# 66 columns of the edge sort on TensorE, attention head by head with its quotients on ScalarE

## What is computed

```
xn = layernorm(x)
# 1. graph part: edge softmax over each source, messages both ways
e     = exp(w - max(w, 0));  row_sum = segment_sum(e, src)
att   = e / (row_sum[src] + 1e-6)
M     = xn @ Wm + bm
out0  = segment_sum(att * M[dst], src);  out1 = segment_sum(att * M[src], dst)
g     = relu(relu(layernorm([out0 out1] @ W1 + b1)) @ W2 + b2), zero where row_sum == 0
# 2. linear attention, 8 heads of 64
q = softmax(xn Wq + bq), k = softmax(xn Wk + bk)  (over the 64 of a head), v = xn Wv + bv
context = k^T v (64 x 64 a head);  D_inv = 1 / (q . sum_t k)
mix = (q context * D_inv + q) @ Wp + bp
x = x + g + mix
# 3. experts: each row goes to one of 8 FFNs (512 -> 256 -> 512, gelu), times its router's probability
x = x + ffn(layernorm(x))
```

## Time and profile before

| | us |
|---|---|
| median of 3 runs (lowest, highest) | 497.45 (495.84, 501.89) |
| the profiled execution's own time | 500.75 |
| its span, first to last instruction | 498.7 |
| PE, PEld busy | 424.8, 347.8 |
| DVE, ACT, POOL busy | 380.7, 266.9, 208.9 |
| TensorE's mean granted clock | 0.955 of full speed |

### The profile page before, as it was taken

One profiled execution on the slowest core, in us unless ns is written; L12 is line 12 of the kernel. 1 busy time (PEld: TensorE's weight loads), 2 busy tenths in 40 slices (PEclk: granted clock), 3 DMA queues, 4 the chain that ended last, 5 costly groups with the idle time before them and its releaser, 6 DMA issues.

```text
span 498.7 us, 8596 instructions
## 1 busy us (share of the span) xinstructions
PE 424.8 (85%) x2637; PEld 347.8 (70%) x2637; DVE 380.7 (76%) x790; ACT 266.9 (54%) x739; POOL 208.9 (42%) x157
## 2 busy tenths in 40 slices
PE   4189999999998999975777777899898857999992
PEld 1167888888877887964555555799876745788881
DVE  6979979999978886963999999478379973455652
ACT  0686667776662222740667777654335661566550
POOL 0588888688886888992000000000000007255322
PEclk9699999999999999995999999999999857999998
DMA  7980000000000000005000000000006964233210
GB/s 196 312 289 3 1 3 3 3 3 2 3 2 3 1 3 2 2 2 185 3 1 2 2 2 1 2 0 1 1 0 258 411 214 126 74 114 111 69 63 17
DMA packets 15584, 31.06 MB, mean 62 GB/s; under 512 B 7494, under 2 KB 8125, under 8 KB 14517
## 3 DMA queue, kind: packets, MB, share of 16 engines
q1 hardware_dynamic: 9237, 23.21, 13.6%
q0 software_dynamic: 6304, 7.30, 7.3%
HBM read 24.90 MB, written 7.37 MB: 65 GB/s over the span
## 4 chain that ended last, share of the span: by engine, by line
PE 36%; POOL 35%; issue 11%; DVE 7%; ACT 5%; DMA 4%; SPq 1%; ACTq 0%; DVEq 0%; POOLq 0%
POOL slots L485 33%; PE banks L733 9%; PE banks L886 7%; PE banks L569 5%; PE banks L752 4%; ACT adj L1601 4%; PE banks L745 2%; DMA x_rows<-factors 2%; PE banks L877 2%; PE banks L702 1%; DVE stat L1337 1%; PE banks L818 1%; PE banks L725 1%; DMA rec<-x_rows,get_i 1%; DVE rec L1335 1%
## 5 line engine op out<-in xcount | busy, mean ns | idle before, releaser
L485 POOL DMA_INDIRECT slots<-record,row_i x112 | 167.3, 1494 | 38.5 <-issue 37.9
L496 POOL DMA_INDIRECT rec<-x_rows,get_i x17 | 18.6, 1092 | 188.8 <-DMA x_rows<-factors 183.9
L1601 ACT ACTIVATE adj<-banks x108 | 58.4, 589 | 39.5 <-PE banks L733 38.2
L569 PE MATMUL banks<-w_hi,xT_hi 128*125 128x512 f32 (+1 forms) x160 | 59.5, 372 | 0.7 <-DVE xT_lo L1088 0.6
L733 PE MATMUL banks<-d_hot,s_hot 128*128 128x251 f16 x432 | 59.9, 276 | 0.2
L569 PE MATMUL banks<-w_lo,xT_hi 128*125 128x512 f32 (+1 forms) x160 | 58.5, 366 | 0.0
L569 PE MATMUL banks<-w_hi,xT_lo 128*125 128x512 f32 (+1 forms) x160 | 58.5, 366 | 0.0
L1536 ACT ACTIVATE q_sb<-q_sb,hmax 125x64 f32<-125x64 f32 x80 | 26.7, 335 | 34.2 <-DVE hmax L1111 34.2
L733 PEld LDWEIGHTS banks<-d_hot,s_hot 128*128 128x128 f16 x432 | 33.4, 97 | 7.3 <-issue 0.3
L569 PEld LDWEIGHTS banks<-w_hi,xT_hi 128*125 128x125 f32 x160 | 29.7, 185 | 7.0 <-ACT xT_hi L1511 0.9
L505 POOL DMA_INDIRECT out<-o_sb,out_i x17 | 17.1, 1006 | 41.4 <-DVE o_sb L1441 41.4
(11 more groups left out here) (300 smaller groups left out, 1062.8 us busy)
## 6 DMA issues: line engine op xcount, KB each, us to landing
w_raw<-in_w2f SPq DMA_DIRECT2D x4, 1024.0 KB, 9.2
w_raw<-in_wqkv SPq DMA_DIRECT2D x3, 1024.0 KB, 17.5
rec<-in_x SPq DMA_DIRECT2D x2, 1120.0 KB
x_rows<-rec SPq DMA_DIRECT2D x10, 224.0 KB
w1a<-in_w1f SPq DMA_DIRECT2D x1, 2048.0 KB, 7.5
w1b<-in_w1f SPq DMA_DIRECT2D x1, 2048.0 KB, 16.5
b_sb<-in_b2f SPq DMA_DIRECT2D x1, 2048.0 KB, 22.2
slots<-record,row_i POOLq DMA_INDIRECT x112
```

Source lines behind the costliest of these rows:

```text
L485: pool.indirect_dma_start(slots, bass.IndirectOffsetOnAxis(ap=row_i[:, c:c + 1], axis=0), record[:, c, :], None).then_inc(slot_st, 16)
L569: mm = pe.matmul(dst, ab, cd, start=(i == 0), stop=(i == n - 1))
L1601: act.activation(adj[:, bass.ds(w, BW2)], flat_banks[0:TP, bass.ds(out_at, BW2)], ACT.Copy).then_inc(win_ok, 1)
```

## The change

- PCOLS goes from 58 to 66: POOL scatters 104 columns, PE sorts 33 pairs of columns instead of 29 (EARLY stays 6).
- k^T v goes head by head: eight matmuls of 64 stationary and 65 moving columns instead of four of 128 and 129. Even heads come out on PSUM partitions 0 to 63, odd ones on 64 to 127, all in bank 7. `ctxd` has 65 columns a head; its zeros go, and one copy on DVE and one on ACT bring it over instead of four each.
- The attention product goes head by head: eight matmuls with contraction 64 and 65 columns; even heads into one bank, odd ones into another.
- The quotients move from DVE to ACT: DVE takes the reciprocals of tile t+2 at the end of the loop of tile t (`attend`), ACT multiplies head by head (`divide`, eight activations of 125x64 out of PSUM a tile), and DVE adds q (`add_query`).
- The bias row and the router's column sums move behind the sort and RUN_UP, into banks 0 and 1, after PE has waited for `part_ok`; DVE takes them up behind its last batch. `wp_raw` therefore has to live longer, and `got`, `keys`, `parts` and `v_sb` get other places; the column of ones in `v_sb` is set once `w_lo` is made.

```diff
-PCOLS = 58
+PCOLS = 66
...
-        v_sb = place("v_sb", 26624, [TP, 2, KD, 129])
+        v_sb = place("v_sb", 5000, [TP, 2, H, DH + 1])
...
+        def ctx_at(h):
+            s = 64 * (h % 2)
+            return bank[7][s:s + 64, h // 2 * (DH + 1):(h // 2 + 1) * (DH + 1)]
+
+        def num_at(t, odd):
+            return bank[((3, 2), (4, 7))[t % 2][odd]][0:TP, 0:KD * (DH + 1)].rearrange("p (k n) -> p k n", k=KD)
...
@@ PE @@
-                for k in range(KD):
-                    kk = k_sb[:, r, k * 128:(k + 1) * 128]
-                    first, last = t == 0 and k == 0, t == NT - 1
-                    mm = pe.matmul(ctx_at(k), kk, v_sb[:, r, k, :], start=first or (t == 0 and k == 3), stop=last,
-                                   skip_group_check=True)
+                for h in range(H):
+                    mm = pe.matmul(ctx_at(h), k_sb[:, r, h * DH:(h + 1) * DH], v_sb[:, r, h, :],
+                                   start=(t == 0 and h < 2), stop=(t == NT - 1), skip_group_check=True)
...
-            bias_row(0)
-            bias_row(1)
             context(NT - 1)
...
             def attend(t):
                 if t >= 2:
                     pe.wait_ge(num_used, t - 1)
-                for k in range(KD):
-                    mm = pe.matmul(num_at(t, k // 2)[:, k % 2, :], qT[:, k, t * TP:(t + 1) * TP],
-                                   ctxd[:, k, :], start=True, stop=True)
+                for h in range(H):
+                    s = slice(64 * (h % 2), 64 * (h % 2) + 64)
+                    mm = pe.matmul(num_at(t, h % 2)[:, h // 2, :], qT[s, h // 2, t * TP:(t + 1) * TP], ctxd[s, h // 2, :],
+                                   start=True, stop=True)
                 mm.then_inc(num_ps, 1)
...
             attend(0)
             attend(1)
-            bias_row(2)
-            bias_row(3).then_inc(row_ps, 1)
             ao_turn(0)
...
             for _ in range(RUN_UP):
                 pe.matmul(bank[IDLE_IN][:, 0:WIN], ident, const("cols"), start=True, stop=True)
+            pe.wait_ge(part_ok, 2)
+            pe.wait_ge(ld_wp, 32)
+            for k in range(KD):
+                pe.matmul(bank[0][0:TP, :], bv_col[:, k:k + 1].to_broadcast([128, TP]), wp_raw[:, k, :], start=(k == 0),
+                          stop=(k == KD - 1))
+            pe.wait_ge(ld_small, 16)
+            for k in range(KD):
+                mm = pe.matmul(bank[1][0:TP, 0:E], ones[:, 0:TP], little("ws")[:, k * E:(k + 1) * E], start=(k == 0),
+                               stop=(k == KD - 1))
+            mm.then_inc(row_ps, 1)
...
@@ DVE @@
             def attend(t):
                 dve.wait_ge(num_ps, t + 1)
                 if t >= 2:
-                    dve.wait_ge(aoT_ps, t - 1)
...
+                    dve.wait_ge(num_used, t - 1)
+                for odd in range(2):
+                    last = dve.reciprocal(rden[:, t % 2, odd, :], num_at(t, odd)[:, :, DH])
+                last.then_inc(rden_ok, 1)
+
+            def add_query(t):
                 dve.wait_ge(num_used, t + 1)
                 dve.tensor_tensor(ao[:, t % 2, :], ao[:, t % 2, :], q_sb[:, t, :], ALU.add).then_inc(ao_ok, 1)
...
+            attend(0)
+            attend(1)
             for t in range(NT):
-                attend(t)
...
+                add_query(t)
                 if t >= 1:
                     aoT_split(t - 1)
...
                 if t >= 2:
                     mix_add(t - 2)
+                if t + 2 < NT:
+                    attend(t + 2)
...
@@ ACT @@
+            def divide(t):
+                act.wait_ge(rden_ok, t + 1)
+                if t >= 2:
+                    act.wait_ge(aoT_ps, t - 1)
+                for h in range(H):
+                    last = act.activation(ao[:, t % 2, h * DH:(h + 1) * DH], num_at(t, h % 2)[:, h // 2, 0:DH], ACT.Copy,
+                                          scale=rden[:, t % 2, h % 2, h // 2:h // 2 + 1])
+                last.then_inc(num_used, 1)
+
+            divide(0)
+            divide(1)
             for t in range(NT):
                 act.wait_ge(aoT_ps, t + 1)
...
+                if t + 2 < NT:
+                    divide(t + 2)
                 if t in SCALED:
                     act_parts(SCALED[t])
```

More of the change, by code:

```diff
@@ L257, in build @@
         hrec = sb("hrec", [TP, 2, H])
-        ctxd = sb("ctxd", [128, 4, 130])
-        rden = sb("rden", [TP, 2, 2, 2])
+        ctxd = sb("ctxd", [128, KD, DH + 1])
+        rden = sb("rden", [TP, 2, 2, KD])
         pr_i = sb("pr_i", [TP, 2, NB], I32)
@@ L290, in build @@
         flat_banks = banks[:, :, :].rearrange("p b n -> p (b n)")
-        def ctx_at(k):
-            return bank[7][:, k * 129:(k + 1) * 129] if k < 3 else bank[2][:, 0:129]
-        def num_at(t, half):
-            return bank[((3, 2), (4, 7))[t % 2][half]][0:TP, 0:260].rearrange("p (k n) -> p k n", k=2)
+        def ctx_at(h):
[3 more added lines that the diff above has]
+            return bank[((3, 2), (4, 7))[t % 2][odd]][0:TP, 0:KD * (DH + 1)].rearrange("p (k n) -> p k n", k=KD)
         def turn_at(n):
@@ L397, in batch_of, with ctx_copy @@
             return n, pair - BATCHES[n][0]
-        def ctx_copies(copy, h):
-            s = slice(64 * h, 64 * h + 64)
-            got = bank[7][s, 0:387].rearrange("p (k n) -> p k n", k=3)
-            copy(ctxd[s, 0:3, s], got[:, :, s])
-            copy(ctxd[s, 0:3, 128 + h], got[:, :, 128])
-            copy(ctxd[s, 3, s], bank[2][s, s])
-            return copy(ctxd[s, 3, 128 + h:129 + h], bank[2][s, 128:129])
+        def ctx_copy(copy, odd):
+            s = slice(64 * odd, 64 * odd + 64)
+            return copy(ctxd[s, :, :], bank[7][s, 0:KD * (DH + 1)].rearrange("p (k n) -> p k n", k=KD))
         block = ctx.enter_context(nc.Block())
@@ L757, in _ @@
             pe.wait_ge(mix_ok, NT)
+            pe.wait_ge(row_ok, 1)
             pe.wait_ge(win_ok, PAIRS)
@@ L1097, in _ @@
                                   w_hi[:, 2 * i:2 * i + 2, WN:WP], ALU.subtract).then_inc(fold_ok, 1)
-            own_step(dve.memset(v_sb[:, :, :, 128:129], 1.0))
+            dve.wait_ge(w_lo_ok, 3)
+            own_step(dve.memset(v_sb[:, :, :, DH:DH + 1], 1.0))
             dve.wait_ge(ld_bias, 16)
@@ L1116, in _ @@
                     xT_split(t + 1)
-                if t == 1:
-                    own_step(dve.memset(ctxd[:, :, :], 0.0))
-                    dve.engine_nop().then_inc(ctxd_zero, 1)
                 if t < 2:
@@ L1155, in attend @@
                 if t >= 2:
-                    dve.wait_ge(aoT_ps, t - 1)
-                for hf in range(2):
-                    last = dve.reciprocal(rden[:, hf, :, :], num_at(t, hf)[:, :, 128:130])
-                own_step(last)
-                for hf in range(2):
-                    last = dve.tensor_tensor(
-                        ao[:, t % 2, hf * 256:(hf + 1) * 256].rearrange("p (k h d) -> p k h d", k=2, h=2),
-                        num_at(t, hf)[:, :, 0:128].rearrange("p k (h d) -> p k h d", h=2),
-                        rden[:, hf, :, :].unsqueeze(3).to_broadcast([TP, 2, 2, DH]), ALU.mult)
-                last.then_inc(num_used, 1)
+                    dve.wait_ge(num_used, t - 1)
[3 more added lines that the diff above has]
+            def add_query(t):
                 dve.wait_ge(num_used, t + 1)
@@ L1262, in _ @@
                 last.then_inc(batch_ok, 1)
+            dve.wait_ge(row_ps, 1)
+            dve.wait_ge(ld_bias2, 16)
+            dve.tensor_copy(ws_sum[:, :], bank[1][0:TP, 0:E])
+            dve.tensor_tensor(bias("p"), bias("p"), bank[0][0:TP, :], ALU.add).then_inc(row_ok, 1)
             dve.wait_ge(win_ok, PAIRS)
@@ L1547, in _ @@
                     act.wait_ge(ctx_ps, t - 1)
-                act.activation(v_sb[:, t % 2, :, 0:128], bank[5][0:TP, :].rearrange("p (k n) -> p k n", k=KD),
+                act.activation(v_sb[:, t % 2, :, 0:DH], bank[5][0:TP, :].rearrange("p (h n) -> p h n", h=H),
                                ACT.Copy).then_inc(v_ok, 1)
@@ L1553, in _ @@
             act.wait_ge(ctx_ps, NT)
-            act.wait_ge(ctxd_zero, 1)
-            ctx_copies(lambda dst, src: act.activation(dst, src, ACT.Copy), 1).then_inc(ctx_ok, 1)
+            ctx_copy(lambda dst, src: act.activation(dst, src, ACT.Copy), 1).then_inc(ctx_ok, 1)
             act.wait_ge(m_ps, NT)
```

31 lines of the change are left out of this document (7 added, 24 removed).

## The result

The changed kernel takes 511.06 us (median of 4 runs, 509.01 to 514.34), the kernel before beside it 498.17 us (4 runs). The ratio is 1.0237 [1.0189, 1.0284]: about 11.8 us slower (the interval says 9.4 to 14.1, the medians themselves lie 12.9 apart), where 6.1 were forecast. The profiled execution has a span of 512.5 us against 498.7; both profiled executions lie about 3 us above the median of their kernel.

A forecast was written before the change was run, and what follows sets the result against it. Two chains, POOL's scatters and PE's sort behind attention, were taken to end close together, with PE's start setting what follows. -3.5 (lighter POOL) + 9.6 (attention) + 0 (context) = +6.1 on 497.45 gave 503.5 us; range 493.5 to 514.

The forecast's parts named there:

- What the moved matmuls free ahead of the sort is nothing.: Ahead of attention: bias row and router sums lay in PE's waits or overlapped DVE's work, so removing them gains 0.
- The order on DVE: Attention: the query addition stands behind reciprocals waiting for a later attend; period 4.09 to 5.5 us, 9.8 over tiles 1 to 7.
- Attend 1.01 a tile: Attention product on PE: 16 head-by-head passes cost about 1.0 us a tile as before, ends 0.5 and 1.89.
- Rival A: Attention: attend's 16 weight loads run one after another, 1.89 us a tile, +8.4 us, time 512; chance 0.27.
- B: Attend and context: both array halves run side by side, 0.5 and 0.48 us a tile, time 494; chance 0.10.
- Context at 0: k^T v over ten tiles: 16 passes, each halved on both sides, cost the same; alternatives +9.2 or -4.9 us.
- the landing of the scatters: POOL: the 104th scatter starts at 197.31 and lands at 201.1, ahead of the end of the sort.
- the run-up: Between sort and windows on PE: follows the sort on a warm clock, 4.3 us instead of 7.26 cold.
- the moved matmuls: Behind the run-up on PE: bias row 3.45 us and router sums 0.95, all on the path.
- D: POOL: the 104th scatter stands until the sort ends; sort to reset 15.3 us instead of 8.7, time 510; chance 0.04.
- the lighter POOL: Up to PE's first reset: fewer scatters and warm run-up, less four sort pairs and the moved matmuls, give -3.5 us.
- C: Attention: DVE's new order costs nothing, -3.5 us, 494; at most -11.9, 485.5, if the sort's end is hidden; chance 0.07.

The follow-up runs named there:

- e3: Changed kernel with bias row and router sums computed and used in their old places, none behind the sort; 505.47 us, ratio 1.0122.
- e2: Changed kernel with four bias-row and four router-sum matmuls also computed in their old places, results unused; 510.52 us, ratio 1.0198.
- e9: Kernel before with 66 columns and only the bias row and router sums moved behind the sort; 495.75 us, ratio 0.9955.
- e5: Changed kernel with DVE's addition and split ahead of the reciprocals, and bias row and router sums back in their old places; 499.54 us, ratio 1.0037.
- e7: e5 with the quotients back on DVE in the order of the kernel before, attend still head by head; 495.41 us, ratio 0.9993.
- e4: Kernel before with 66 columns on PE instead of 58, nothing else changed; 494.36 us, ratio 0.9919.
- e8: e4 with k^T v head by head, attend as in the kernel before; 492.83 us, ratio 0.9931.
- e6: Changed kernel with 58 columns on PE again instead of 66; 507.62 us, ratio 1.021.
- e12: e8 with 64 columns on PE instead of 66; 488.73 us, ratio 0.9789.
- e1: Changed kernel with DVE's next query addition and the split moved ahead of the reciprocals, ACT still dividing; 506.54 us, ratio 1.0126.
- e11: e9 with k^T v head by head as well, attention as in the kernel before; 495.46 us, ratio 0.9935.

## Why the prediction was right and wrong

The direction was right and the range (493.5 to 514) held the time, but the size was off by half: +6.1 was forecast and +11.8 measured (by the ratio), so most of the chance lay on a change within 2%, and the measured one is about that or slightly over it (2.4%, interval 1.9 to 2.8).

**The step that failed** is the sentence "What the moved matmuls free ahead of the sort is nothing." It looked at the freed time alone, found that it lay in PE's waits, and priced it at zero. In this kernel those matmuls kept PE at full clock through two waits for DVE. Without them, and with the shorter k^T v, the clock went to half until 166 us, some 13 us, at the price of 4.1 us between first and fourth attend (14.3 after, 10.2 in e3; the other 1.0 us of the 5.1 missed there is lost at full clock too). With them back in place the clock is 1.00 (e2, e3). What is shown is this step from after to e3; why the clock stayed full in e9 stays open. I had noticed a cold run-up at 0.68 in the rows of before and asked about the clock there, and not at the place from which work was taken.

**What attention costs, by one part undone after the other** (stage times; each step is a run):

| from | to | what is undone | us |
|---|---|---|---|
| after 61.1 | e3 57.0 | fillers back in front: the clock | -4.1 |
| e3 57.0 | e5 50.5 | reciprocals ahead of the addition on DVE's queue | -6.5 |
| e5 50.5 | e7 47.6 | quotients on ACT, with the order that goes with them | -2.9 |
| e7 47.6 | e4 46.0 | attend head by head | -1.6 |

**The order on DVE**: right in mechanism and close in size. The period was walked at 5.5 us and is 5.68. PE's idle time in front of ao_turn, released by DVE's addition, is 1.07 (walked 1.24). Two small errors nearly cancel: the hand-over is 0.23 shorter, and the switch between half and whole array, 0.32, was not in the sum. I had charged all of this to the order; e5 to e7 shows that 2.9 us of it would stay with e5's order, since reciprocal, eight activations and addition are a longer chain than the same on one engine.

**Attend 1.01 a tile** was right: 16 loads in 0.95. Rival A is refuted at full clock. 16 passes of 125 columns at 0.118 would be 1.89; even and odd heads load side by side, 0.059 a pass. That A's 512 lies next to the measured 511.06 is chance: its place, ten attends, shows nothing. B's side-by-side attend of 0.5 isn't there either.
The Trainium skill ("TensorE: Matmul & The Clock Gate", LDWEIGHTS) says that a load's time goes by its columns whatever its rows. The records agree: a load of attend with its 64 rows lasts 185 ns (mean of 48 between 183 and 200 us), the whole-array loads of `mix_out` beside it 185 to 186, and a load of a single row (L527) 181. So half the rows don't make the load shorter; the loads only start 0.059 us apart instead of 0.118, and two loads to different halves of the rows share their time.

**Context at 0** was a little high: 0.55 instead of 0.97 us of loads a tile, of which 0.9 us in all (e4 to e8; 1.0 from before to after) reach the first attend. The tables of stages hide it behind the later start of the projection.

**The sort, the landing of the scatters, the run-up, the moved matmuls, the windows stage**: +3.85 against +3.85; the 104th scatter started at 197.01 against 197.31 and nothing stood still, so D did not occur; sort to reset 8.3 against 8.7; windows 81.14 against 80.9. e4 shows the lighter POOL alone at 7.8 to `rs`, e3 the moved matmuls at 4.2 of that given back. C (the hand-over costs nothing) is refuted by the period.

**Where the gain of the lighter POOL went**: it was there, 7.8 us, and 4.2 of it were given back at once by work put on PE, which paces everything behind the sort; the remaining 3.6 stand against an attention stage that is 15.2 longer (the sum is 11.6, the +11.6 to `rs`). And e6 shows that with such a stage the lighter POOL is not even needed.

## What to carry to other kernels

Work that fills an engine's waits isn't free to move: it may be holding up the clock for what follows, so look at PE's busy time on either side of the place it leaves, and price the next stretch at both levels. In a queue written by hand, an operation that another engine waits for goes ahead of a wait for that engine's later product; moving a step to an engine with spare time can lengthen the chain by two hand-overs and a slower form of the step (2.9 us of attention here). And when two chains end together, try the part that shortens one of them by itself: here 66 columns alone gave 0.8% (e4), 64 with the narrower k^T v 2.1% (e12, of which 3.9 us lie in a stretch that no edit touches), and the rest of the change took it all away.

## What the hardware showed that was not expected

- Two PE waits of 1.60 and 1.27 us, with PE busy for 1.47 of the 4 us ahead of the first attend, were followed by half clock, as in e1, e6 and e11 (1.47, 1.46, 1.46); with waits of 1.33 and 1.28 us and 1.65 of 4 busy it stayed full in e9's one profile. What tips it stays open. The clock came back after 3 us in a dense stretch (e11) and after 13 in one with waits (after).
- Loads of 125 columns for different row halves of the array start every 0.059 us in alternation, against 0.118 for the whole array, though each lasts 185 ns in either case; a pass of 64 loaded columns in k^T v 0.55 / 16 = 0.034.
- A load for half the array waits for the pass of the whole array ahead of it, 0.32 us a tile; a whole-array load behind half-array ones doesn't (e7).
- POOL's scatters pass beside DVE's gapless sort in some places (e12's 106th, 1.42 us, begun 2.4 us into the sort) and stand for 19.00 us in another (before's 107th, begun 4.15 us into it). What decides it wasn't tried.
